# Cross-attention and mixture-of-experts block: half-height transposes for one pair of turns, and four projected tiles one unit later

## What is computed

```python
# ctx_1024: (4, 77, 256), x: (4, 1024, 256), 16 heads of 64
xn, ln = layernorm(ctx_1024), layernorm(layernorm(x))
q  = (ln @ Wq)                                   # 1024 queries
kv = concat([xn @ Wkv, ln @ Wkv], axis=1)        # 77 + 1024 keys and values
sim = einsum('bhid,bhjd->bhij', rmsnorm(q) * scale, rmsnorm(k))
attn = softmax(where(mask, sim, -max))
x = x + einsum('bhij,bhjd->bhid', attn, v) @ Wout + bout
x = x + shared_mlp(layernorm(x)) + sum_of_top_2_of_8_expert_mlps(layernorm(x))
```

## Time and profile before

| | us |
|---|---|
| median of three runs | 2508.64 |
| the profiled execution, whole | 2505.31 |
| its span, first to last instruction | 2503.8 |
| PE matmuls busy | 2408.4 |
| ACT busy | 1689.1 |
| DVE busy | 1749.3 |
| POOL busy | 1212.2 |
| one window of attention (start of unit 4's scores to the next) | 50.1 |

### The profile page before, as it was taken

The page is one execution under the profiler, slowest core; times in us unless marked ns, Lnnn a source line. Parts: engine busy times, 40 slices in busy tenths (PEclk is TensorE's granted clock), DMA queues, the critical chain, the costliest instruction groups (busy, mean ns, idle before and its releaser), DMA issues. The chain is left out here.

```text
span 2503.8 us, 53762 instructions
## 1 busy us (share of the span) xinstructions
PE 2408.4 (96%) x19926; PEld 1997.1 (80%) x19926; DVE 1749.3 (70%) x2452; ACT 1689.1 (67%) x2286; POOL 1212.2 (48%) x783
## 2 busy tenths in 40 slices
PE   4899999999999999999999999988989999999997
PEld 3677777777777777777777777658989999999997
DVE  7666766676667666766676667777875567777775
ACT  2688888888888888888888888872333345444443
POOL 5444434443445344534453445425515537677766
PEclk9899999999999999999999999998999999999999
DMA  6423332323333323233333232247804279999996
GB/s 199 148 84 115 100 98 86 124 92 100 94 115 100 101 85 123 91 100 94 115 99 101 86 123 90 68 125 167 200 10 144 92 243 320 317 327 317 319 326 166
DMA packets 231532, 363.25 MB, mean 145 GB/s; under 512 B 59559, under 2 KB 139739, under 8 KB 227400
## 3 DMA queue, kind: packets, MB, share of 16 engines
q1 hardware_dynamic: 204694, 301.66, 39.2%
q0 software_dynamic: 25696, 58.82, 8.1%
q10 hardware_dynamic: 978, 0.34, 0.1%
HBM read 280.90 MB, written 79.85 MB: 144 GB/s over the span
## 5 line engine op out<-in xcount | busy, mean ns | idle before, releaser
L734 DVE TENSOR_TENSOR pr_lo<-ps_s,pr_hi 128x1024 fp32r<-128x1024 f32 x420 | 513.0, 1221 | 297.2 <-ACT ps_s L844 297.2
L843 ACT ACTIVATE pr_hi<-ps_s 128x1024 fp32r<-128x1024 f32 x512 | 527.4, 1030 | 133.5 <-PE ps_s L991 110.1
L476 POOL TENSOR_TENSOR rs<-ss,minus_half 128x16 f32<-128x16 f32 (+1 forms) x96 | 226.8, 2362 | 555.4 <-DVE ss L709 555.4
L1700 ACT ACTIVATE ht<-f_ps_h,b 128x256 f32<-128x256 f32 x440 | 184.6, 471 | 338.8 <-PE f_ps_h L1632 338.8
L1027 PE MATMUL ps_o<-pr_hi,vA 64*65 64x512 f32 x1780 | 378.2, 391 | 2.5 <-DVE pr_lo L734 2.5
L1027 PE MATMUL ps_o<-pr_lo,vA 64*65 64x512 f32 x1780 | 377.2, 390 | 0.0
L1027 PE MATMUL ps_o<-pr_hi,vC 64*65 64x512 f32 x1780 | 376.5, 390 | 0.0
L844 ACT ACTIVATE ps_s<-ps_s 128x1024 f32<-128x1024 f32 x360 | 370.9, 1030 | 0.0
L1632 PE MATMUL f_ps_h<-xT_hi,w 128*128 128x256 f32 x1760 | 353.5, 284 | 3.3 <-DVE xT_lo L1734 2.3
L957 PE MATMUL ps_m<-w_sb,lnT_sb 64*128 64x384 f32 (+1 forms) x3072 | 326.0, 335 | 11.7 <-POOL w_sb L532 4.8
L1645 PE MATMUL f_ps_y<-w,h_hi 128*128 128x256 f32 x1760 | 325.6, 283 | 0.0
(11 more groups left out here) (220 smaller groups left out, 4698.3 us busy)
## 6 DMA issues: line engine op xcount, KB each, us to landing
w<-w1S_dram SPq DMA_DIRECT2D x160, 512.0 KB, 6.2
lnT_sb<-lnT_dram SPq DMA_DIRECT2D x31, 2304.0 KB, 8.9
w2raw<-in_L_ffn_Wproj SPq DMA_DIRECT2D x78, 512.0 KB, 7.0
w1S_dram<-cut POOLq DMA_DIRECT2D x36, 512.0 KB, 3.0
rec<-rden_dram SPq DMA_DIRECT2D x63, 256.0 KB, 3.7
routed_dram<-empty POOLq DMA_DIRECT2D x28, 387.0 KB, 3.5
xt<-routed_dram SPq DMA_DIRECT2D x39, 258.0 KB, 6.7
w_raw<-in_L_xattn_Wkv SPq DMA_DIRECT2D x66, 128.0 KB, 2.9
```

Of the source, the lines that this page charges most:

```text
L476: g.tensor_tensor(rs[:, 0:sums], ss[:, 0:sums], minus_half[:, 0:sums], ALU.pow).then_inc(s_pool, 1)
L734: v.tensor_tensor(pr_lo[:, ring(w, d), :], full_of(w, d), pr_hi[:, ring(w, d), :].bitcast(F32), ALU.subtract).then_inc(s_lo, 1)
L843: act.activation(pr_hi[:, ring(w, d), :], ps_s[:, d % 2, :], ACT.Exp, bias=bias)
L1700: ins = act.activation(ht[:, p, i, :], ps_h[:, p % 2, i, :], ACT.Gelu_apprx_tanh, bias=b1[:, slot, p, i:i + 1])
```

## The change

Three edits, all in PE's program or in a table that ACT reads as well:

1. Turns 2 and 3 at unit 4 (`CUT`) become sixteen transposes of 64 rows by 128 columns in place of eight whole ones (`turn_halves`). Each transpose of one turn is paired with one of the other on the other 64 rows and in the other bank. Eight of them (part 0) come ahead of unit 4's `first`, eight (part 1) behind it. The turns' waits all stand ahead of part 0, and both turns are told ready at the end of part 1.
2. Tiles 0 and 1 are projected at unit 7 in place of 6, tiles 2 and 3 at unit 9 in place of 8. ACT's copies move with them.
3. PE's general version is written out straight in place of a loop.

```diff
-PROJECTED = {6: (0, 1), 8: (2, 3), 11: (4,), 13: (5, 6), 15: (7, 8)}
-HALVED = (6, 8, 13, 15)
+PROJECTED = {7: (0, 1), 9: (2, 3), 11: (4,), 13: (5, 6), 15: (7, 8)}
+HALVED = (7, 9, 13, 15)
+CUT = 4
...
+            def turn_halves(w, turns, part):
+                for i in turns:
+                    if part == 0:
+                        turnable(w, i)
+                if part == 1:
+                    pe.wait_ge(s_turnhalf, w.n(1, 2))
+                for k in range(MOST_TILES):
+                    for j, i in enumerate(turns):
+                        kind, first, stop = PARTS[i]
+                        at, row = 2 if kind == "k" else 0, DH * (j ^ part)
+                        rows = slice(row, row + DH)
+                        ins = nc.tensor.transpose(ps_m[:, (1 + i) % 2, k * P + row:k * P + row + DH],
+                                                  nrm[rows, first + k, at:at + 2, :].rearrange("p j d -> p (j d)"), ident[rows, rows])
+                        if part == 1 and k == MOST_TILES - 1:
+                            ins.then_inc(s_job, 1)
+                if part == 0:
+                    ins.then_inc(s_turnhalf, 1)
...
+                        elif w.turn and d == CUT:
+                            turn_halves(w, TURNED[d], 0)
+                            first(d)
+                            turn_halves(w, TURNED[d], 1)
...
-                if general:
-                    windows(pe, window)
-                else:
-                    for v in range(-1, WINDOWS // 2):
-                        for s in range(2):
-                            window(Window(v, s))
+                for v in range(-1, WINDOWS // 2):
+                    for s in range(2):
+                        window(Window(v, s))
```

More of the change, by code:

```diff
@@ L227, in attention @@
         s_scores, s_exp, s_lo, s_pv = t.sem("a_scores"), t.sem("a_exp"), t.sem("a_lo"), t.sem("a_pv")
-        s_o, s_half, s_jobhalf = t.sem("a_o"), t.sem("a_half"), t.sem("a_jobhalf")
+        s_o, s_half, s_jobhalf, s_turnhalf = t.sem("a_o"), t.sem("a_half"), t.sem("a_jobhalf"), t.sem("a_turnhalf")
         s_mx, s_red, s_shift = t.sem("a_mx"), t.sem("a_red"), t.sem("a_shift")
@@ L905, in _, with turnable @@
             pe.wait_ge(s_const, 6)
-            def turn(w, i):
-                out = ps_m[:, (1 + i) % 2, :]
+            def turnable(w, i):
                 kind, first, stop = PARTS[i]
-                at = 2 if kind == "k" else 0
                 if i < 2:
@@ L917, in turn @@
                 pe.wait_ge(s_nrm, w.n(GROUPS, GROUPS + -(-stop // MOST_TILES)))
+            def turn(w, i):
+                turnable(w, i)
+                out = ps_m[:, (1 + i) % 2, :]
+                kind, first, stop = PARTS[i]
+                at = 2 if kind == "k" else 0
                 for k, tile in enumerate(range(first, stop)):
```

## The result

| | before | after |
|---|---|---|
| median, 14 runs each | 2508.90 us | 2513.49 us |
| lowest to highest | 2506.53 to 2511.03 | 2510.01 to 2520.71 |
| profiled execution, whole | 2505.31 | 2511.53 |
| its span | 2503.8 | 2510.0 |

The ratio is 1.0021, with a 95% interval from 1.0013 to 1.0029: 0.2% slower, or about 5 us. The forecast was 2512.6 us, with 2508 to 2518 as the range.

The account below looks back on a forecast made before the run. Bound: PE, nearly gapless, plus the ACT and DVE chain whose `pr_lo` releases unit 7's scores. Terms 3.9 + 0.3 - 0.2 = +4.0 us took the median from 2508.64 to 2512.6 us; range 2508 to 2518 us.

Parts of the forecast that it names:

- Price of the halves: Unit 4's turns: sixteen 64-row transposes take 0.5 us instead of 1.17 us, saving PE 0.67 us a window.
- Rival B: Unit 4's turns: each half transpose costs as much as a whole, 1.75 us for sixteen; +20.5 us, 2529 us; chance 0.06.
- Removed wait for `q_lo`: At unit 6's projection, PE no longer waits for DVE's `q_lo`: PE saves 0.32 us a window.
- The chain: ACT's exps and copies of units 4 and 5, then DVE's `pr_lo`, hold unit 7's scores until about 7.2 us after unit 4's.
- The size per window: Each projecting window gets 0.13 us longer, times 30 is +3.9 us; bounds 0 and 0.2 us a window.
- Rival A: In the windows only PE's time counts: 30 x 0.99 = 30 us saved, 2479 us; chance 0.04.
- Rival D: The new `pr_lo` wait costs no more than the old, and the opening gives back what it takes: 2508.6 us; chance 0.12.
- The straight version: PE's general version doesn't run; the plain version jumps over more code once: 0, at most +0.5 us.
- The opening: Projection queued behind batch 1's transposes delays the second opening window 2 us, partly regained; attention starts +0.3 us, bounds -0.5 and +3.
- rival C: Opening: PE's new idle stretch could halve its clock and slow the projection behind it; +3 us, 2515.6 us; chance 0.20.
- The first attending window: Its projection starts later now, and the window may gain 0.2 us.
- My sign of being wrong: Wrong if attention starts over 1.5 us late, unit 8's scores come before 11.3 us, or halves take over 1.2 us.

Follow-up runs that it names:

- the longer and the shorter chain: One more ACT copy: changed kernel 2526.8 us, kernel before 2508.2 us; changed kernel with turn 3's copies behind unit 5's exps and `pr_lo`: 2500.1 us.
- copy_split: Changed kernel with turn 3's ACT and DVE copies moved behind unit 5's exps and `pr_lo`; 2500.1 us, ratio to the kernel before 0.9958.

## Why the prediction was right, and where it was not

**The forecast and its sign.** 2512.6 us against 2513.5. It holds because the steady term was right, and the steady term rested on one question asked of the rows: when this wait goes, what is late next? That the total came within 1 us is luck in part: the same kernel measured again gave 2514.7 us, and the small terms beside the steady one were not as forecast.

- *Price of the halves*: 0.46 us against 0.5 taken and 0.45 as the lower end. Rival B, halves as dear as wholes, is out: each half's load does take as long as a whole's, but the loads overlap (see the last section), and B needed that they didn't.
- *Removed wait for `q_lo`*: gone in the changed kernel; back, and longer, in the one with the halves alone.
- *The chain*: unit 7's scores 7.17 us after unit 4's, forecast 7.17. Its place and its one-to-one effect are shown by the longer and the shorter chain.
- *The size per window*: +0.13 us taken, +0.15 measured, +4.3 us between the marks in place of 3.9 - 0.2 = +3.7.
- *Rival A*, that PE alone counts (30 us), is out: from 102 to 1605 us PE is busy 10 us less, and the windows there are longer.
- *Rival D*, the new wait as cheap as the old, is out for the windows: both profiles of the changed kernel and the one of the move show 50.24 us or more. Its other half, that the opening gives back what it takes, is what the three groups of starts above show.
- *The straight version*: nothing measurable.

**What was off.**

- *The opening.* The gap, the slower projection behind it that rival C named, and the 2 us at the second opening window came as described (that projection ended at 41.05 and 41.99 us, not near 40). But the second window gives back more than that, so that the changed kernel is early by about 0.7 us where the two orders meet again, at 86 us; I had it late by 0.3, with 0.5 early as the bound. The 0 to 4.5 us that are lost behind it go with the granted clock, in kernels old and new. My sign of being wrong, attention more than 1.5 us late, can't be read from one profile: 105.33 is late beside 102.28, but the straight kernel is at 105.37.
- *The first attending window*, -0.2 us, can't be told: it took 50.41 us in the profile of before, 49.93 in the straight kernel's, 50.21 and 50.25 in the two of after.
- *Rival C* is therefore right in its mechanism for the opening and unproven in its price. Less the 4.3 us, the ratios leave -1 to 3 us by the first measurement and 0.5 to 6.5 us by the second; no run shows whether the clock falls more often after the change.
- *The end.* I had no term for what follows the marks, nearly all of it code that the change doesn't touch. From the closing window's unit 4 to the end it took 898.4 us in the profile of before, 901.3 and 899.2 in the two of after, and 903.5 in the straight kernel's. Over all twelve profiles it is 898.0 to 903.5, in the mean 901.0 in the three kernels with turns and projections as before and 900.8 in the other nine, so it is no cost of the change. It is also why the first two profiles differ by 6.2 us: -1.0 ahead of the marks, +4.3 between them, +2.9 behind. PE's granted clock in this stretch differs from one execution to the next; 1860 to 1900 us, before and in the straight kernel:

```profile
1860.00:1900.00 40.00, 39.25 (x331) 1.00 0.17 61
```

```profile
1860.00:1900.00 40.00, 39.25 (x313) 0.94 0.14 47
```

- *PE's busy time* was to fall by 20 us and fell by 7.4. Idle moments shorter than the 0.4 us for which an earlier matmul is recorded don't count as idle (0.61 us of standing still at unit 7 are recorded as 0.41), and a first pair after a wait is recorded 0.1 us longer.

## What to carry to other kernels

An engine that is busy 96% of the span isn't thereby the only bound: lay the engines' timelines over one period, and for each buffer that is handed back and forth write down when the slower side gives it back, counted from a common start. Removing a wait, or cheapening work in front of one, moves the wait to the next of those times; here unit 7's scores could come 2.07 us earlier and no more, while the projection that had moved behind them takes 4.18 - 2.07 = 2.11 us and a first weight load shows once more. The gain lay in the order of two copies, one on ACT and one on DVE, busy 67% and 70% of the time, and it cost no instruction. The two were moved together; what each is worth alone was not tried.

## What the runs showed of the hardware

- Transposes of 64 rows by 128 columns with 64 columns moving run in pairs every 0.05 us (eight in 0.21 us), recorded 222 ns long against 273 ns for whole ones, and pass to 64-row matmuls and back without the 0.1 us that 128-row work costs at each end. Doubling the number of weight loads cost nothing that shows. The Trainium skill ("TensorE: Matmul & The Clock Gate", section "LDWEIGHTS (loading the stationary operand)") says that a load costs the same for fewer rows. The loads here agree: 138 ns in the median for 64 rows and 140 for 128. As the halves' pairs follow each other every 0.05 us, their loads must overlap.

Loads before; loads and transposes after (count, then shortest, median and longest in ns):

```profile
L919 PEld LDWEIGHTS ps_m<-a_ident,nrm x544: 137/140/231, 51.9 to 1626.1; 128*128 128x128 f32 x182
```

```profile
L939 PEld LDWEIGHTS ps_m<-a_ident,nrm x512: 134/138/222, 64.3 to 1610.8; 64*128 64x128 f32 x171
L939 PE MATMUL ps_m<-a_ident,nrm x512: 213/222/367, 64.4 to 1610.9; 64*128 64x64 f32 x171
```

- With PE waiting three times in each window of the changed kernel the granted clock was 1.00 from 102 to 1605 us. In the closing window of `copy_split` it was 0.66 from 1606 to 1611 us, right behind PE's wait of 2.65 us; with the old first opening window besides, the wait is 2.67 us and the clock stayed at 1.00, so the wait alone doesn't decide it.
- From 86 us to unit 4 of the first attending window the twelve profiles take 16.13 or 16.14 us where the granted clock from 86 to 104 us is 1.00, 17.6 where it is 0.91, 18.3 to 19.1 at 0.81, 19.7 and 19.8 at 0.72, and 20.6 at 0.62. The end varies by some 5 us as well, and both do so in kernels that run the same code there. For a change worth 0.2%, marks inside the steady part tell more than a single span.
